# A third row pair computed with seven products for eight, with all engine orders rewritten and idle transposes ahead of the first product

## What is computed

```python
bm = mask.reshape(Nb, BH, Kb, BW).sum(axis=(1, 3)) > 0      # 32 x 32 blocks
w  = weight with the blocks of bm kept, the others zero
xn = layernorm(x)
s  = einsum('bsk,nk->bsn', xn, w) + bias
coeffs = softmax(q @ lora_keys.T / sqrt(128)),  q = xn.mean(axis=1) @ Wq.T
h  = einsum('bsi,eir->bser', xn, lora_down)
g  = silu(einsum('bsi,oi->bso', xn, W_org) + einsum('be,bser,ero->bso', coeffs, h, lora_up))
out = x + s * g
```

## Time and profile before

| | |
|---|---|
| time of three runs | 434.46, 432.40, 432.04 us, median 432.4 us |
| span of the profiled execution, first to last instruction | 437.0 us |
| TensorE matmuls busy | 417.0 us, 95% |
| VectorE busy | 384.2 us, 88% |
| ScalarE busy | 241.2 us, 55% |
| GpSimd busy | 54.3 us, 12% |
| DMA | 110.51 MB, 253 GB/s over the span |

### The profile page before, as it was taken

The page is one execution under the profiler, slowest core; times in us unless marked ns, Lnnn a source line. Parts: engine busy times, 40 slices in busy tenths (PEclk is TensorE's granted clock), DMA queues, the critical chain, the costliest instruction groups (busy, mean ns, idle before and its releaser), DMA issues. The chain is left out here.

```text
span 437.0 us, 6104 instructions
## 1 busy us (share of the span) xinstructions
PE 417.0 (95%) x1857; PEld 336.3 (77%) x1857; DVE 384.2 (88%) x592; ACT 241.2 (55%) x427; POOL 54.3 (12%) x61
## 2 busy tenths in 40 slices
...
PEclk9699999999999999999999999999999899999999
...
GB/s 304 400 397 174 142 150 301 303 220 301 270 272 284 326 202 255 353 352 333 325 302 199 95 74 244 174 375 348 315 366 336 271 44 177 59 241 230 170 232 200
DMA packets 46176, 110.51 MB, mean 253 GB/s; under 512 B 4800, under 2 KB 7104, under 8 KB 45376
## 3 DMA queue, kind: packets, MB, share of 16 engines
...
...
## 5 line engine op out<-in xcount | busy, mean ns | idle before, releaser
L1005 PE MATMUL psA<-b_hi,a_hi 128*128 128x512 f32 (+1 forms) x444 | 173.9, 392 | 1.4 <-ACT snaps L1273 0.9
L1007 PE MATMUL psA<-b_hi,a_lo 128*128 128x512 f32 (+1 forms) x444 | 172.1, 388 | 0.0
L1006 PE MATMUL psA<-b_lo,a_hi 128*128 128x512 f32 (+1 forms) x444 | 172.0, 387 | 0.0
L1005 PEld LDWEIGHTS psA<-b_hi,a_hi 128*128 128x128 f32 x444 | 83.4, 188 | 21.1 <-ACT snaps L1273 2.2
L1007 PEld LDWEIGHTS psA<-b_hi,a_lo 128*128 128x128 f32 x444 | 83.4, 188 | 17.3
L1006 PEld LDWEIGHTS psA<-b_lo,a_hi 128*128 128x128 f32 x444 | 83.4, 188 | 16.3
L1388 DVE TENSOR_TENSOR b_lo<-b_raw,b_hi 128x512 fp32r<-128x512 f32 (+2 forms) x78 | 59.7, 790 | 0.0
L1229 ACT ACTIVATE b_hi<-b_raw 128x512 fp32r<-128x512 f32 (+2 forms) x66 | 44.8, 717 | 21.7 <-DVE b_raw L1395 7.8
L1273 ACT ACTIVATE snaps<-psA 128x512 f32<-128x512 f32 x39 | 23.0, 590 | 35.2 <-PE psA L1007 35.2
L1215 ACT ACTIVATE a_hi<-s_raw 128x512 fp32r<-128x512 f32 x52 | 31.7, 623 | 15.6 <-DVE s_raw L1379 13.9
L1388 DVE TENSOR_TENSOR a_lo<-s_raw,a_hi 128x512 fp32r<-128x512 f32 x52 | 35.1, 688 | 1.0 <-ACT a_hi L1215 0.8
...
## 6 DMA issues: line engine op xcount, KB each, us to landing
...
```

Source lines behind the costliest of these rows:

```text
L1005: nc.tensor.matmul(ps, l_hi, r_hi, start=first, stop=False, skip_group_check=True)
L1006: nc.tensor.matmul(ps, l_hi, r_lo, start=False, stop=False, skip_group_check=True)
L1007: return nc.tensor.matmul(ps, l_lo, r_hi, start=False, stop=over, skip_group_check=True)
```

## The change

`WFIRST` becomes 2, so that pair 2 is done with seven products and there are 114 products in place of 115. The transposition of tiles 4 and 5 on TensorE stays (a new constant `TXP` = 3 takes over that role). The first seven-product groups begin with (2,1), (2,2), (3,1), (3,2), so that the products with T1 to T4 come later. All five lists are rewritten. In TensorE's list, `CP0` stands ahead of the transposes of tile 0, and two new steps `F0.30 F1.14` issue 44 transposes of the identity between tile 0's transposes and P0. In SyncE's list, `LM0` is issued first. The number of other steps changes by: 3 `H`, 3 `QS` and 1 `QO` more on ScalarE; 3 `V`, 4 `S`, 2 `PB` more and 1 `QC` less on VectorE. The diff below is cut to its core; of the lists it shows, from the top, lines of SyncE's (the start, the E stretch of b = 0, that of b = 1), the starts of TensorE's and ScalarE's, four lines of VectorE's, and the start of GpSimd's.

```diff
-WFIRST = 3
+WFIRST = 2
+TXP = 3
...
-        if u in SETS:
+        if u == WFIRST:
+            order += [(u, 1), (u, 2), (u + 1, 1), (u + 1, 2), (u, 5), (u, 6), (u, 7), (u, 4), (u, 3)]
+        elif u in SETS:
...
-    LX0 LX2 LM0 LX1 LX3 LW0.0 LW0.1 LM1 LX4 LW1.1 LW1.0 LM2 LM3 LI LW2.0 LK LY LX5 RS2 LW3.0 ST2 RS0 LX6 LX8 RS1 RS4
+    LM0 LX0 LX3 LW0.0 LX2 LW0.1 LX1 LM1 LW1.1 LX4 LW1.0 LM2 LM3 LI LX5 LK RS1 LY LW2.0 RS0 LW3.0 RS3 RS2 LX6 LX7 LT6
...
-    LE0.1.2 LE0.2.0 LD0.2.1 LE0.3.0 LD0.3.1 LD0.3.2 ST55 LD0.2.3 ST57 LG9.0 LE0.2.1 LD0.2.2 LB0 LB2 LE0.3.3 LE0.3.1
-    LE0.2.3 LE0.2.2 RS15 LB3 LD0.3.3 LG10.0 LE0.3.2 LG9.1 LR0 LR1 LR2 LG10.1 LB1 LR3 LG11.0 LB4 ST60 LR5 ST64 LR4
...
+    LE0.3.0 LE0.2.1 LE0.2.0 LD0.3.3 ST55 LE0.3.1 RS15 LD0.3.2 LD0.2.2 LD0.2.3 LE0.3.3 LE0.2.3 LE0.2.2 LE0.3.2 LG10.0
+    LG9.0 ST57 LG9.1 LR0 ST56 LB3 LB0 LR2 LB1 LR1 LB2 LG10.1 LB4 LB7 ST59 LR4 LB6 LR3 ST64 ST63 LG11.0 LB5 LG11.1 LR6
...
-    LG11.1 ST66 LB6 ST67 ST65 LB7 LR6 LB8 LB5 LB10 LB9 ST70 LR8 LR9 LR7 ST72 LG12.0 LB12 LR10 LG12.1 ST73 LU1.1.0
-    LR11 LB11 LU1.1.1 ST77 LU1.7.0 ST74 LU1.7.1 LR13 LB14 LD1.0.0 LU1.3.0 LB13 LU1.3.1 ST80 ST79 LR12 LR14 LU1.2.0
-    LB15 LU1.2.1 LD1.0.1 LD1.1.0 LE1.0.0 LD1.1.2 LD1.1.1 LR15 LE1.1.0 LD1.1.3 LD1.0.3 LD1.0.2 LE1.0.1 LD1.3.0
-    LE1.1.1 LE1.0.3 LD1.2.0 LE1.1.3 LE1.0.2 ST83 ST84 LG13.0 LE1.1.2 LD1.2.2 LE1.3.0 LE1.2.0 LD1.3.1 LD1.2.1 LE1.3.1
...
+    LU1.7.0 LU1.7.1 LU1.3.0 LB13 LR13 ST76 LU1.3.1 LD1.0.3 LD1.1.0 LU1.2.0 LB14 ST78 LU1.2.1 LD1.0.0 LD1.1.3 LD1.0.2
+    LD1.0.1 ST79 LD1.1.1 LE1.0.0 LR14 LR15 LB15 LE1.1.0 LE1.0.1 LD1.1.2 LE1.0.3 LE1.1.1 LE1.1.3 LE1.0.2 LD1.2.0 LE1.1.2
+    LD1.2.1 LD1.3.0 LE1.3.0 LE1.2.0 LD1.3.1 LE1.3.1 LE1.2.1 ST85 LD1.3.2 LD1.2.2 LE1.2.3 LD1.2.3 LE1.3.3 LE1.2.2
...
-    TX0.0 TX0.1 CP0 P0 TX1.0 TX1.1 CP1 TX2.0 TX2.1 P1 P2 CP2 TX3.0 P3 TX3.1 K P4 CP3 TX4.0 P5 TX4.1 P6 P7 P8 P9 P10
+    CP0 TX0.0 TX0.1 F0.30 F1.14 P0 TX1.0 CP1 TX2.0 TX1.1 TX2.1 P1 P2 P3 CP2 TX3.0 TX3.1 P4 K P5 CP3 P6 TX4.0 P7 TX4.1
...
-    TC0.0 CA0.0 TC0.1 H4 H6 HB0.0.2 CA1.1 CA1.0 TC1.0 H2 H0 TC1.1 HB0.0.0 HB0.0.3 HB0.1.0 CA2.1 CA2.0 TC2.0 TC2.1
+    CA0.0 TC0.0 TC0.1 HB0.0.2 CA1.1 CA1.0 TC1.0 HB0.0.0 TC1.1 H4 H0 H5 HB0.1.0 CA2.1 H2 CA2.0 CA3.0 TC2.1 HB0.1.1
...
-    SN0 SN2 LN0.0 CA0.1 SN1 CB0 CM0 SN3 W0.1 W0.2 W0.3 LN1.1 LN2.0 LN2.1 V4 CB1 CM1 SN4 V2 V0 R1 W1.1 LN3.0 LN3.1
-    R0 VB0.7.0 V5 V6 VB0.2.0 QC6 QC7 R3 T0.0.3 V8 LN5.0 V10 V7 T0.0.1 V9 T0.0.2 T0.0.4 QC12 VB0.4.0 QC14 V11 R4
-    VB0.6.0 N6 QC13 R5 N7 R6 S3.2 N8 S3.3 QC15 R7 QC18 QC19 V12 N9 VB0.3.0 V13 V14 QC22 V15 QC23 BD V16 DT0.1 R8
-    PB3.1 GA0 DT0.4 S4.1 VB0.5.0 V17 V19 V18 S4.3 V20 S4.2 DT0.3 N10 S4.4 QC28 N11 VD0 V21 QC31 V23 V22 V26 N12 V25
...
+    CA0.1 SN0 CB0 CM0 LN0.0 SN3 W0.1 SN2 W0.2 SN1 W0.3 R0 LN2.0 LN2.1 LN3.0 CB1 LN1.1 CM1 SN4 R1 W1.1 V0 VB0.0.2
+    QC3 V6 VB0.7.0 QC6 V7 R2 V5 VB0.2.0 T0.0.3 R3 QC7 R4 T0.0.1 PB2.0 N6 T0.0.2 S2.1 V8 S2.3 QC12 VB0.3.0 V9 S2.2 V11
+    QC13 T0.0.4 QC15 S2.4 QC14 V10 V14 BD N7 V12 PB2.1 VB0.4.0 V15 V13 S3.2 VB0.5.0 VB0.6.0 N8 R6 QC22 V16 V17 S3.3 R5
...
-    SR0 LN0.1 SR2 SR1 W0.0 LN1.0 W1.0 SR4 SR3 W3.0 XR6 SR5 LN5.1 XR8 XR7 XR9 S3.1 XR11 XR10 S3.4 XR12 DT0.2 XR13
+    SR0 LN0.1 W0.0 SR1 SR2 LN1.0 SR3 W1.0 SR5 LN5.1 SR4 W3.0 XR6 XR7 XR8 XR9 XR10 S3.1 XR12 S3.4 XR11 DT0.2 XR13 XR14
...
-            if t // 2 < WFIRST:
+            if t // 2 < TXP:
...
-                if kind == "CP":
+                if kind == "F":
+                    for _ in range(st[2]):
+                        nc.tensor.matmul(psA[:, ACC - 1, 0:P], ident[:, :], ident[:, :], start=True, stop=True,
+                                         is_transpose=True)
+                elif kind == "CP":
...
-                    if t < 2:
+                    if t < 2 or t >= 2 * WFIRST:
```

More of the change, by code:

```diff
@@ L64, in products @@
     for u in range(WFIRST, GROUPS):
-        if u in SETS:
+        if u == WFIRST:
+            order += [(u, 1), (u, 2), (u + 1, 1), (u + 1, 2), (u, 5), (u, 6), (u, 7), (u, 4), (u, 3)]
+        elif u in SETS:
             order += [(u, 1), (u, 2), (u, 5), (u, 6), (u + 1, 1), (u, 7), (u + 1, 2), (u, 4), (u, 3)]
         elif u + 1 < GROUPS and u + 1 not in SETS:
-            order += [(u, 1)] if u == WFIRST else []
-            order += [(u, 2)] if u - 1 not in SETS else []
+            order += [(u, 2)] if u - 1 not in (*SETS, WFIRST) else []
             order += [(u, 6), (u, 5), (u, 7), (u + 1, 1), (u, 4), (u, 3)]
@@ L125 @@
-    ST111 ST112 ST113 TS0 TS1
-    """,
-    """
-    TX0.0 TX0.1 CP0 P0 TX1.0 TX1.1 CP1 TX2.0 TX2.1 P1 P2 CP2 TX3.0 P3 TX3.1 K P4 CP3 TX4.0 P5 TX4.1 P6 P7 P8 P9 P10
-    P11 TX5.0 TX5.1 P12 BP6 P13 P14 P15 P16 BP7 BP8 P17 P18 BP9 P19 P20 P21 P22 P23 BP10 BP11 P24 P25 P26 P27 BP12
-    BP13 P28 P29 P30 P31 BP14 P32 P33 P34 P35 P36 P37 BP15 G0 P38 P39 P40 P41 P42 P43 P44 P45 P46 P47 P48 P49 P50
-    P51 P52 P53 P54 P55 P56 G1 P57 P58 E0.0.1 E0.1.1 E0.0.2 E0.1.2 E0.0.6 E0.1.6 E0.0.5 E0.1.5 E0.0.7 E0.1.7 E0.0.4
```

123 lines of the change are left out of this document (67 added, 56 removed).

## The result

The kernel after takes 458.8 us (median of 4 runs, 457.0 to 460.3) beside 433.4 us for the kernel before on the same chip (432.0 to 436.7): ratio 1.0592, 95% interval 1.0551 to 1.0633. The forecast was 428.9 us. The change loses some 25 us where 3.5 were to be won. One execution of b3, its profiled one, took 704.4 us at a mean granted clock of 0.56; it is left out of b3's ratio, and its trace is not read.

A forecast was written before the change was run, and what follows sets the result against it. TensorE was taken to bound the kernel, with VectorE nearly always busy too. Against the median 432.4: -2.7 - 1.1 + 1.0 - 1.0 - 0.5 + 0.8 = -3.5, giving 428.9 us, range 425.3 to 432.8.

The forecast's parts named there:

- for these and for new meetings in 290 DMA issues: SyncE's order in the E stretches: down-weight loads now behind other loads, and other new meetings, cost +0.8 us, bounds 0 and 3.
- The prediction's own sign of being wrong: TensorE in the two E stretches: more than 5 us of waits there would show the prediction wrong.
- VectorE's bill: VectorE gets 4.8 us more work where 91 to 98% busy; expected cost to the time +1.0 us, bounds 0 and 4.6.
- VectorE becomes the bound: Rival: the whole 4.6 us of VectorE's added work is paid in place of 1.0, giving 432.5 us; chance 0.12.
- The place named for it: First narrow place, T3's low part for product (2,7), P22: due at 87.0, ready at 89.3, stall 0 to 2.3 us.
- The product: Pair 2 on TensorE: seven products for eight, 12 matmuls less at 0.227 us each, -2.7 us.
- The opening: Start of the kernel: P0 at 16.2 to 17.4 at full clock, P1 at 21.9 for 23.03, -1.1 us.
- the rival in which the clock falls and comes back midway in the transposes: Opening: the clock falls, returns midway in the 44 transposes, costing 1.7 us more, 430.6 us; chance 0.11.
- the second gate: Ahead of P1: steps behind the count of mask block 1 let P1 start not before 21.5 us.
- The rival that all transposes run cold and hold P0 up to 21.3: Opening: 44 transposes at 0.23 us take 10.1, P0 starts at 21.3, +7.3 us, 436.2 us; chance 0.05.
- SyncE in the E stretches: SyncE's load order in the E stretches: fewer waits, -1.0 us in batch 0, -0.5 in batch 1 against the median.
- The two waits named: E stretches: TensorE's 1.76 us behind `LE0.3.1` in batch 0 and 2.93 us behind `LD1.2.1` in batch 1 go.

The follow-up runs named there:

- b3: Changed kernel with VectorE's differences of down-weight blocks 2 and 3 moved behind other VectorE steps; ratio 1.0624 to the kernel before.
- a4: Changed kernel without the 44 idle transposes; ratio 1.0558 to the kernel before.
- c3: Changed kernel with early edits alone: three GpSimd operations given to VectorE, tile 5's row sum and two stores earlier, six low parts placed first; ratio 1.0587.
- b4: Changed kernel's orders up to 125 us of its trace, the orders of the kernel before from there on; ratio 1.0352.
- c4: Changed kernel's orders up to 400 us of its trace, the orders of the kernel before from there on; ratio 1.0490.
- a3: Changed kernel's orders up to 202 us of its trace, the orders of the kernel before from there on; ratio 1.0419.
- c1: b4 without the idle transposes, with the early edits of c3 and two VectorE low parts at the seam moved ahead; ratio 1.0190.
- e2: c1 with eight more steps moved in the orders of ScalarE, VectorE and SyncE; ratio 1.0105, 436.8 us.
- a1: Changed kernel with most of GpSimd's array work cut to a few columns, places and waits kept; ratio 1.0455.
- b1: Changed kernel with eight VectorE operations, two sums and six low parts, cut to 8 of 512 columns; ratio 1.0656.
- a2: Kernel before with most of GpSimd's array work cut to a few columns, as in a1; ratio 0.9965.
- d1: Changed kernel with VectorE's drains (result copies out of accumulator banks) of products 41 and 48 moved earlier in its order; ratio 1.0787.
- e1: d1 with six stores of drained results issued earlier in SyncE's order; ratio 1.0675.
- f1: e1 with steps of the down-weight block chain moved ahead on VectorE, ScalarE and SyncE, by order alone; ratio 1.0656.

## Why the prediction was wrong

**The step that failed is the last term of SyncE's part, "for these and for new meetings in 290 DMA issues: +0.8, bounds 0 and 3".** It priced the rewriting of five lists of 1471 steps as a few meetings on one queue in the E stretches. With the seven-product pair kept and other orders, the ratio went from 1.0592 to 1.0105, so orders hold about 21 us of the 25 (without the transposes, and with three GpSimd steps given to VectorE, neither of which won anything clear of noise by itself in a4 and c3). 10.4 of it came back in b4, where nothing but order differs. They act everywhere: 4.4 us in the tail (c4), which the sum took as it was; 3.1 from 202 to 400 us (a3 less c4); 2.9 from 125 to 202 (b4 less a3), with the cost of the seam taken off; 7.0 ahead of 125 and at the seam (c1 less b4); and 3.7 by eight steps more (e2 less c1). The 3.1 and the 2.9 are each within the noise of two ratios. These 21 us and the 5.9 of a1 are not two bills: the stretched time of VectorE, 15.2 us in the kernel after, is 9.4 in b4 and 4.4 in e2. The prediction's own sign of being wrong came as well: TensorE is idle for 5.9 us in the two E stretches, where it allowed 5.

**VectorE's bill, +1.0 with bounds 0 and 4.6.** The count was right: the trace has 8 instructions more, and cutting eight of them short took some 4.2 us of work off in b1 (0.16 for 0.68 us each). The bound was wrong, because it held durations and waits constant. Stretching beside GpSimd adds 12.2 us to VectorE's busy time; without it 5.9 us of the time come back in a1, 1.5 in the kernel before (a2). And the whole bill of 4.6 is no upper bound when VectorE has no slack and stands in its order behind loads: 5.9 us of waits for down blocks, where the trace before had 1.4. That "VectorE becomes the bound" was priced at 432.5 is the same error. The place named for it was right as a beginning: P18, P21 and P32 idled 0.2 to 0.8 us and began 0.1 behind their low parts. P22, the product that the prediction named, found its low part done 0.8 us before (at 90.96 for the 89.3 foreseen) and idled 0.7 for something else: ScalarE's snapshot of P21. Products 6 and 7 of pair 2 now follow each other directly, and the 0.7 stands in the best of the orders (e2) too. No term of the sum has it.

**The product, -2.7: as stated.** 12 matmuls less, in steps of 0.227. In the whole it cannot be seen by itself: e2, the best order found for it, is 4.5 us slower than the kernel before, so either it costs 7 us in waits or its order is still not found. Which of the two stays open.

**The opening, -1.1.** P0 came at 17.55 (16.2 to 17.4 foreseen) and was 3.60 us long. What came is the rival in which the clock falls and comes back midway in the transposes: the 44 took 6.19 us for 5.1, since the first of them ran at the low clock. P1 came at 22.87 for 21.9, so this term gave 0.16 and not 1.1. In a4, without the transposes, P1 came at 21.49, where the prediction had put the second gate (21.5): the gate, and not P0's clock, was the limit, so the transposes could win nothing there. The lead of 2.0 at P4, of which 1.7 was the key product, was lost by P8, which idled 1.14 us for the low part `VB0.7.0`, behind the stretched one of 3.54. The rival that all transposes run cold and hold P0 up to 21.3 did not come.

**SyncE in the E stretches, -1.0 and -0.5.** The two waits named are gone, and `b_hi` costs 2.2 us for 4.0. Others took their place (`b_raw` L1403, 3.0 us in three). The stretch of b = 0 takes 42.9 us for 41.3, that of b = 1 42.8 for 44.4. So where 1.0 was to be won at b = 0, 1.6 was lost. At b = 1 1.6 came of the 4.6 counted against the profiled span.

**What stays open.** Which meetings, one by one, make up the 6 us that the new orders lose between 138 us and the E stretch. d1, e1 and f1 took away, one after the other, two drains' places, their stores' places and parts of the down chain's order, and P51 came at 188.2, 184.0 and 184.2 for 182.2. In the kernel after, the drain and the low part that P51 needs lie 0.6 us apart; that more chains lie as close is likely, but not shown.
